# Softmax maxima as two rows of the stacked queries, a layer norm's affine folded into the next weights, and a new order of the steps

## The chip, the cores and the metric

The kernel runs on one core of one Trainium2 chip. The metric is the device time in microseconds, the median of the runs; one further execution was profiled, and all rows below come from it.

## The reference

Eight images of 256 channels and 16 x 16 pixels pass three blocks. The window block (two window attentions, one of them on DCT coefficients, then a 1x1 and a 3x3 convolution and a batch norm over all images) is the first half of the kernel. What the change touches is the second half. There `t` is an image as 256 tokens of 256 channels:

```python
out = feat + relu(batchnorm(y))                     # per image, t = out as tokens
mu, var = t.mean(-1), ((t - mu) ** 2).mean(-1)
tn = (t - mu) / jnp.sqrt(var + EPS) * n3_w + n3_b   # the MLP's affine
h = jax.nn.gelu(tn @ fc1_w.T + fc1_b, approximate=False)
t = t + (h @ fc2_w.T + fc2_b)
# attention, 16 heads of 16, rotary, causal, on the layer norm of t
scores = jnp.einsum('bhqd,bhkd->bhqk', q, k) * scale
probs = jax.nn.softmax(jnp.where(causal, -jnp.inf, scores), axis=-1)
t = t + (probs @ v) @ w_out
# eight experts, the two best by the gate's logits, on the layer norm of t
t = t + sum(combine[:, e] * (x @ expert_w[e].T) for e in range(8))
```

## The kernel before

Products of float32 quality are made from float16 parts: each operand is split into a high part (a cast, on ScalarE) and a low part (operand minus high part, on VectorE or GpSimd), and three matmuls are summed (`split_products`, line 200).

`windows` is the first half, up to about 345 us. At three of its steps it scales and splits the weights of the second half in chunks (`act_weights`, `dve_weights`). `images` is the second half. Each engine has its own in-order program; semaphores join them. The order in which each engine meets the steps comes from one list, made by `image_order` out of two tables written by hand: `MLP_SLOT` and `IMAGE_SLOT`. An entry is a step's name and its lag in slots; the steps of a slot follow the table, and each engine takes from the list those steps that it has a part in.

The steps of the MLP for image c: `load` (batch norm, relu, sum with the input), `tokens` (transpose, statistics on VectorE, `deviation` on GpSimd), `mlp_normalise` (ScalarE, two activations), `mlp_channels` (transposes on TensorE; on ScalarE two affine activations with `n3w`, `n3b` into `wide`, then the high part), `mlp_low`, `widen` (fc1, gelu, split of the hidden values on ScalarE and GpSimd), `narrow` (fc2), `mlp_base` (adds the bias of fc2). All eight images' MLPs run ahead of the first `attend`; the first steps of the attention of images 0 to 2 are interleaved with the last of them ("the fill").

The attention of image c: `qkv_normalise`, `qkv_channels`, `qkv_low`; `rotate` j = 0, 1 (products for queries and keys, rotary parts `rot` and `turned` on VectorE); `stack`: GpSimd adds (`rot`, line 1277), ScalarE makes `rh`, GpSimd `rl` (line 1281), SP writes both to `rope_scratch` in HBM and reads them back with twelve transfers (line 946) into `qs[p]` and `ks[p]`, whose rows 0 to 47 then hold high, low and high parts; rows 48 to 79 are zero. `maxima` n = 0..11 makes masked scores of query rows in bank (1, 1) (lines 1051, 1054) and reduces them on VectorE (line 1367); one bank serves all twelve, so each waits for the reduce before it. `shifts` splits the maxima in two bf16 parts (three operations on VectorE) and transposes them; `shift_rows` copies them to `shift[p]`. `attend` gr = 0..3 makes the transposed scores of four heads in three banks; for each head it subtracts the maximum by a second product of a matrix of selectors `headb` with `shift` (lines 1077 to 1084); ScalarE takes Exp (line 1216). `split` makes the parts of the exponentials (ScalarE, and GpSimd at line 1287), `weigh` multiplies with the values. Then `out_channels`, `out_split`, `out_project`, `moe_statistics`, `moe_normalise`, `norm_channels`, `logits` (the gate) and `expert` 0 to 7.

In the steady slots an engine's list holds `attend` of image k, `maxima` of image k + 1, `rotate` and `stack` of image k + 2 and the experts of image k - 1. On TensorE a slot before reads: `shifts`, `qkv_channels`, `attend` 0, `out_project`, `maxima` 0, `attend` 1, `maxima` 1 and 2, `rotate` 0, `maxima` 3, `norm_channels`, `attend` 2, `logits`, `rotate` 1, and then experts, `maxima`, `weigh` and `values` in turns, up to `expert` 7, `weigh` 3, `out_channels`. GpSimd's list: `moe_statistics`, `split` 0, `split` 1, `stack`, `rotated_low`, `split` 2, `split` 3. ScalarE's: `attend` 0, `split` 0, `attend` 1, `moe_normalise`, `split` 1, `norm_channels`, `attend` 2, `logits`, `attend` 3, `stack`, `split` 2, `split` 3 and the rest. SP's: `stack` of k + 2, `store` of k - 1.

## Time and profile before

| | us |
|---|---|
| median of 3 runs | 778.35 |
| lowest, highest | 772.43, 779.28 |
| the profiled execution | 771.87 |
| its span, first to last instruction | 769.9 |
| TensorE (PE) busy | 631.3 |
| VectorE (DVE) busy | 498.6 |
| ScalarE (ACT) busy | 326.8 |
| GpSimd (POOL) busy | 208.5 |

Busy time is a sum over stages with different limits. The page of the profile also has a chain: the work that ended last, followed back step by step to what released it. The granted clock is the share of TensorE's full 2.4 GHz that it was given; it has two levels, 0.5 (1.2 GHz) and 1. Matmuls are pipelined, so where they follow each other their starts tell what one costs.

### The profile page before, as it was taken

To read this page: it belongs to the slowest core of one execution; us is meant where nothing else is said; L and a number is where in the kernel's file an instruction comes from. 1 tells how busy PE (TensorE), PEld (TensorE's weight loads), DVE (VectorE), ACT (ScalarE), POOL (GpSimd) and SP (SyncE) were. 2 spreads that over 40 slices of the span, in tenths; PEclk is the share of its full clock that TensorE was granted. 3 is DMA by queue.
4 is the path that set the end of the run, shared out by engine and by line. 5 is a ranking of instruction groups with operands and counts; after the bars stand their busy time and mean duration, and the time that the engine had idled before them with its cause. 6 is when DMAs were issued, how large, how long until landed. Compare 5 with 4: busy or idle time off the path is not lost.

```text
span 769.9 us, 20275 instructions
## 1 busy us (share of the span) xinstructions
PE 631.3 (82%) x8800; PEld 531.5 (69%) x8800; DVE 498.6 (65%) x1102; ACT 326.8 (42%) x510; POOL 208.5 (27%) x193
## 2 busy tenths in 40 slices
PE   6656999897979897782797766799989898989867
PEld 5545787786868686661685645677878787867655
DVE  3586877878787979314364353477767686857445
ACT  4334434444443444104895224463545445342610
POOL 1000000000000000004587334463737363533330
PEclk9858999999999999995998988799999999999988
DMA  7103110101010000002033031404041322320000
GB/s 267 52 27 103 35 39 16 39 15 39 16 39 2 3 2 3 1 1 68 29 70 62 7 59 12 69 15 70 30 56 37 48 45 40 54 31 15 2 14 14
DMA packets 28408, 29.77 MB, mean 39 GB/s; under 512 B 1952, under 2 KB 22688, under 8 KB 28192
## 3 DMA queue, kind: packets, MB, share of 16 engines
q1 hardware_dynamic: 28320, 28.49, 16.6%
q8 instruction: 69, 1.13, 0.6%
q14 instruction: 19, 0.16, 0.1%
HBM read 22.19 MB, written 6.29 MB: 37 GB/s over the span
## 4 chain that ended last, share of the span: by engine, by line
PE 21%; DMA 10%; DVE 7%; POOL 6%; ACT 6%; SPq 3%; issue 2%; DVEq 0%; POOLq 0%; ACTq 0%
PE ps L200 11%; DMA ks<-rope_scratch 8%; SPq L946 3%; DMA rope_scratch<-rl 2%; PE ps L1051 2%; POOL rot L1277 2%; PE ps L1077 2%; POOL rl L1281 2%; PE ps L1080 2%; DVE mx L1367 1%; PE ps L1099 1%; POOL hl L1273 1%; ACT wide L1187 1%; PE ps L1083 1%; PE ps L962 1%
## 5 line engine op out<-in xcount | busy, mean ns | idle before, releaser
L1287 POOL TENSOR_TENSOR e2l<-prob,e2h 128x1536 f16<-128x1536 f32 x32 | 98.9, 3102 | 26.4 <-ACT e2h L1222 26.2
L1367 DVE TENSOR_REDUCE mx<-ps 128x2 f32<-128x512 f32 (+1 forms) x96 | 65.5, 682 | 33.0 <-PE ps L1054 33.0
L200 PE MATMUL ps<-secondh,ch_moe 128*128 128x256 f16 (+1 forms) x320 | 82.7, 266 | 3.3 <-DVE cl_moe L1320 3.0
L200 PE MATMUL ps<-secondl,ch_moe 128*128 128x256 f16 (+1 forms) x320 | 83.0, 266 | 0.0
L200 PE MATMUL ps<-secondh,cl_moe 128*128 128x256 f16 (+1 forms) x320 | 82.9, 266 | 0.0
L506 PE MATMUL ps<-yh,wconvh 128*128 128x256 f16 x288 | 80.8, 280 | 2.3 <-DVE yl L802 2.3
L506 PE MATMUL ps<-yh,wconvl 128*128 128x256 f16 x288 | 80.8, 280 | 0.0
L506 PE MATMUL ps<-yl,wconvh 128*128 128x256 f16 x288 | 80.4, 279 | 0.0
L1216 ACT ACTIVATE prob<-ps 128x1536 f32<-128x1536 f32 x32 | 46.5, 1452 | 58.5 <-PE ps L1083 58.5
L632 POOL TENSOR_TENSOR rstd<-mv,eps 128x4 f32<-128x4 f32 x8 | 1.6, 201 | 256.4 <-DVE mv L684 256.4
L1457 DVE SCALAR_TENSOR_TENSOR acc<-ps,gate,acc 128x256 f32<-128x256 f32 x112 | 49.0, 479 | 21.9 <-PE ps L200 21.9
L1051 PE MATMUL ps<-ks,qs 80*128 80x128 f16 (+1 forms) x256 | 38.5, 254 | 26.1 <-DVE mx L1367 16.4
L580 ACT ACTIVATE prob<-prob 128x1024 f32<-128x1024 f32 x16 | 16.9, 1058 | 86.0 <-DVE prob L747 86.0
L1222 ACT ACTIVATE e2h<-prob 128x1536 f16<-128x1536 f32 x32 | 47.0, 1476 | 4.8 <-PE ps L1099 3.9
L1051 PEld LDWEIGHTS ps<-ks,qs 80*128 80x128 f16 x256 | 18.6, 100 | 39.8 <-DVE mx L1367 25.6
L1077 PE MATMUL ps<-qs,ks 80*128 80x256 f16 (+1 forms) x256 | 40.0, 260 | 2.3 <-DVE shift L1388 1.1
L1080 PE MATMUL ps<-shift,headb 128*128 128x256 bf16 (+1 forms) x256 | 39.8, 260 | 0.0
L572 ACT ACTIVATE qkh<-ps,sbqk 128x256 f16<-128x256 f32 x64 | 26.9, 471 | 27.6 <-PE ps L200 27.6
L1251 POOL TENSOR_TENSOR rstd<-mv,eps 128x2 f32<-128x2 f32 x24 | 4.7, 196 | 122.4 <-DVE mv L1314 122.4
L200 PEld LDWEIGHTS ps<-secondh,ch_moe 128*128 128x128 f16 x320 | 31.1, 99 | 9.0 <-DVE cl_moe L1320 3.8
L1138 ACT ACTIVATE ch_moe<-ps 128x512 f16<-128x512 f32 x16 | 9.5, 595 | 62.3 <-PE ps L962 62.2
L200 PE MATMUL ps<-xh,wqkh 128*128 128x256 f16 x128 | 35.0, 274 | 0.0
(217 smaller groups left out, 2082.5 us busy)
## 6 DMA issues: line engine op xcount, KB each, us to landing
weights_stage<-in_second SPq DMA_DIRECT2D x6, 684.0 KB, 4.4
qs<-rope_scratch SPq DMA_DIRECT2D x48, 64.0 KB
ks<-rope_scratch SPq DMA_DIRECT2D x48, 64.0 KB
weights_stage<-in_wconv SPq DMA_DIRECT2D x6, 384.0 KB, 4.3
xw<-in_xw SPq DMA_DIRECT2D x8, 256.0 KB, 2.7
xc<-in_xc SPq DMA_DIRECT2D x8, 256.0 KB, 2.6
rope_scratch<-rh SPq DMA_DIRECT2D x8, 256.0 KB, 2.3
rope_scratch<-rl SPq DMA_DIRECT2D x8, 256.0 KB, 2.4
```

The lines of the kernel that those rows point to most:

```text
L200: last = nc.tensor.matmul(out_ap, lhs[x], rhs[w], start=done == 0, stop=done == n - 1)
L506: last = nc.tensor.matmul(bank(p, 2 + oh)[:, 0:TOK], w["wconv"][:, c0:c0 + P], im[:, h, dy:dy + HW, dx:dx + HW], start=(tap, h, n) == (0, ...
L572: nc.scalar.activation(qkh[p][:, j, oh, :], bank(p, j)[:, oh * TOK:(oh + 1) * TOK], ACT.Identity, bias=sbqk[:, j * 2 + oh:j * 2 + oh + 1]) ...
L946: sp.dma_start(dst[p][r0:r0 + 8], src).then_inc(stacked[p], 16)
L1051: nc.tensor.matmul(to[:, m * keys:(m + 1) * keys], qs[p][:, gr * GH + h, q0:q0 + P], ks[p][:, gr * GH + h, 0:keys], start=m == 0, stop=False)
L1077: nc.tensor.matmul(to[:, n * width:(n + 1) * width], ks[p][:, gr * GH + h, k0:k0 + P], qs[p][:, gr * GH + h, q0:TOK], start=n == 0, stop=F ...
L1080: nc.tensor.matmul(to[:, n * width:(n + 1) * width], headb[:, gr * GH + h, :], shift[p][:, q0:TOK], start=False, stop=False)
L1216: nc.scalar.activation(prob[n % 2][:], bank(0, 0, 3), ACT.Exp, scale=SOFTMAX_SCALE).then_inc(exp2, 1)
L1222: nc.scalar.activation(eh[n % 2][:], prob[n % 2][:], ACT.Copy).then_inc(e2_hi, 1)
L1287: nc.gpsimd.tensor_tensor(el[n % 2][:], prob[n % 2][:], eh[n % 2][:], ALU.subtract).then_inc(e2_lo, 1)
L1367: nc.vector.tensor_reduce(mx[c % 2][:, q0 // P, h0:h0 + len(heads)], bank(1, 1).rearrange("p (h m) -> p h m", m=keys), op=ALU.max, axis=AX ...
L1457: nc.vector.scalar_tensor_tensor(acc[c % 2][:, t, :], back_bank(e)[:, t * C:(t + 1) * C], gate[:, t, e:e + 1], (t3 if e == 0 else acc[c % ...
```

## The change

1. `qs` and `ks` get two more rows. Rows 80 and 81 of `ks` hold the constant 2^15. VectorE makes from the transposed maxima two float16 rows per head, -max / 2^15 and what that leaves (`shift_high`, `shift_done`), and SP copies each with one transfer into row 80 or 81 of `qs[p]`. `attend` contracts over 82 rows and has no product with `headb` any more; `headb`, the splitting of the maxima and their operations are gone. `attend` 0 now waits for the two transfers (`shift_in`). `maxima` takes rows 0 to 79 as before.
2. The MLP's affine: the rows of the fc1 weights are multiplied by `n3w` when they are split in `windows`, and `n3b` goes through fc1 once into a bias `fc1bias`, with a load of the raw weights and eight matmuls of one column at the start of `images`. `mlp_channels` on ScalarE is only the high part, read from PSUM. `mlp_normalise` moves from ScalarE to VectorE, as one subtract-and-multiply, and two of GpSimd's small operations go.
3. Both tables of slots are new. In the steady slots TensorE's list becomes: `shifts`, `qkv_channels`, `expert` 7, `out_channels`, `out_project`, `attend` 0, `maxima` 0 and 1, `rotate` 0, `attend` 1, `maxima` 2, `norm_channels`, `maxima` 3, `attend` 2, `logits`, `rotate` 1, `maxima` 4, and then the rest in turns. ScalarE: `attend` 0, `split` 0, `moe_normalise`, `attend` 1, `norm_channels`, `attend` 2, `split` 1, `logits`, `stack`, `split` 2, `attend` 3. GpSimd keeps its order. SP: `shift_rows` of k + 1 comes after `stack` of k + 2. In the MLP the steps of an image are one slot closer together; in the fill, `stack` of image 1 comes ahead of `widen` of image 7 on GpSimd.

```diff
 MLP_SLOT = [
-    ("load", 0), ("widen", 4), ("mlp_normalise", 2), ("mlp_base", 2), ("mlp_low", 3), ("narrow", 5),
-    ("statistics", 5), ("tokens", 1), ("mlp_channels", 2)]
-FILL_FROM, FILL_SLOT, FILL_END = 4.25, 3.0, 30.75
+    ("load", 1), ("mlp_base", 3), ("statistics", 6), ("tokens", 2), ("widen", 4), ("mlp_channels", 3),
+    ("mlp_normalise", 2), ("mlp_low", 3), ("narrow", 5)]
+FILL_FROM, FILL_SLOT, FILL_END = 4.5, 2.75, 18.5
...
+                    for c0, c1_, by in scaled_parts(c, width):
+                        last = nc.scalar.activation(high[:, c0:c1_], stage[slot][:, c0:c1_], ACT.Identity, scale=by)
...
+            def shift_rows(c):
+
+                p = c % 2
+                freed(sp, weights2, (c - 1) * GROUPS)
+                sp.wait_ge(shift_done, c + 1)
+                for n in range(2):
+                    sp.dma_start(qs[p][KROWS + n:KROWS + n + 1], shift[n][p][:]).then_inc(shift_in[p], 16)
...
-                    pe.wait_ge(shift_done, c + 1)
+                    pe.wait_ge(shift_in[p], (c // 2 + 1) * 2 * 16)
...
-                    for n, h in enumerate(heads):
-                        nc.tensor.matmul(to[:, n * width:(n + 1) * width], headb[:, gr * GH + h, :],
-                                         shift[p][:, q0:TOK], start=False, stop=False)
...
-                for h in range(HALVES):
-                    nc.scalar.activation(wide[c % 2][:, h, :], bank(0, 1)[:, h * TOK:(h + 1) * TOK], ACT.Identity,
-                                         scale=col("n3w", h), bias=col("n3b", h)).then_inc(affine2, 1)
-                act.wait_ge(affine2, c * 2 + 2)
-                nc.scalar.activation(ch[MLP][c % 2][:], wide[c % 2][:, 0:2, :], ACT.Copy).then_inc(mlp_hi, 1)
+                nc.scalar.activation(flat(ch[MLP][c % 2]), bank(0, 1), ACT.Copy).then_inc(mlp_hi, 1)
...
+                    last = nc.vector.tensor_scalar(tn[MLP][c % 2][:, t, :], t1[c % IN_MLP][:, t, :],
+                                                   mv[MLP][:, c, t, 0:1], rstd[MLP][:, c, t:t + 1], ALU.subtract,
+                                                   ALU.mult)
...
+                nc.vector.tensor_scalar(shift[0][p][:], bank(1, 1)[0:L1H, 0:TOK], -1.0 / SHIFT, None, ALU.mult)\
+                    .then_inc(shift_high, 1)
+                dve.wait_ge(shift_high, c + 1)
+                nc.vector.scalar_tensor_tensor(shift[1][p][:], bank(1, 1)[0:L1H, 0:TOK], -1.0 / SHIFT, shift[0][p][:],
+                                               ALU.mult, ALU.subtract).then_inc(shift_done, 1)
```

## Rows read from the trace of the kernel before

**Rows 1.** The page's chain that ended last, by line: share of the span.
```profile
PE ps L200 11%; DMA ks<-rope_scratch 8%; SPq L946 3%; DMA rope_scratch<-rl 2%; PE ps L1051 2%; POOL rot L1277 2%; PE ps L1077 2%; POOL rl L1281 2%; PE ps L1080 2%; DVE mx L1367 1%; PE ps L1099 1%; POOL hl L1273 1%; ACT wide L1187 1%; PE ps L1083 1%; PE ps L962 1%
```

**Rows 2.** Busy time by stage: stretch, its length, engines' busy us, clock, DMA.
```profile
core 0: us, PE busy (x) PEld busy (x) DVE busy (x) ACT busy (x) POOL busy (x), PEclk, DMA share, GB/s
348.00:427.00 79.00, 52.22 (x398) 43.22 (x399) 36.23 (x89) 56.66 (x108) 50.49 (x75) 0.83 0.26 57
427.00:459.00 32.00, 24.11 (x183) 18.64 (x182) 16.58 (x38) 5.36 (x9) 11.19 (x16) 0.87 0.18 31
...
496.60:677.00 180.40, 169.48 (x2169) 143.87 (x2168) 133.78 (x336) 84.51 (x88) 90.20 (x50) 0.99 0.28 45
...
712.70:769.90 57.20, 42.47 (x472) 35.02 (x472) 26.89 (x78) 15.63 (x17) 14.80 (x12) 0.85 0.03 10
```

**Rows 3.** The chain inside one slot, 549 to 586: start us, us, what.
```profile
549.15 0.67 DVE turned L1353 x2
549.89 2.37 POOL rot L1277
...
555.63 2.64 DMA rope_scratch<-rl
...
562.33 10.30 DMA ks<-rope_scratch
...
572.68 0.40 PE ps L1051 x4
...
576.73 1.32 PE ps L200 x12
...
585.07 0.76 DVE turned L1353 x2
```

**Rows 4.** TensorE's instructions in order of time, one `attend` and the next `maxima`.
```profile
605.15 0.38 PE L1080 MATMUL ps<-shift,headb 128*128 128x256 bf16 x2
605.37 0.27 PE L1083 MATMUL ps<-laterb,identb 128*128 128x256 bf16 x1
...
608.97 0.40 PE L1051 MATMUL ps<-ks,qs 80*128 80x128 f16 x4 [0.80 <-DMA ks<-rope_scratch]
```

**Rows 5.** DMA issues: count, KB each, median us from issue to landing.
```profile
xc<-in_xc SPq DMA_DIRECT2D x8, 256.0 KB, 2.6
...
out<-acc SPq DMA_DIRECT2D x8, 256.0 KB, 4.9
```

**Rows 6.** The page's costliest groups: busy us, mean ns, idle before, releaser.
```profile
L1287 POOL TENSOR_TENSOR e2l<-prob,e2h 128x1536 f16<-128x1536 f32 x32 | 98.9, 3102 | 26.4 <-ACT e2h L1222 26.2
...
L1216 ACT ACTIVATE prob<-ps 128x1536 f32<-128x1536 f32 x32 | 46.5, 1452 | 58.5 <-PE ps L1083 58.5
```

**Rows 7.** ScalarE's groups of instructions in the MLP, 373 to 403 us.
```profile
L1143 ACT ACTIVATE tn_mlp<-t,centre,rstd 128x256 f32<-128x256 f32 x9 | 4.9, 585 | 0.0
L1177 ACT ACTIVATE wide<-ps,vec 128x256 f32<-128x256 f32 x8 | 4.1, 558 | 2.4 <-POOL hl L1273 2.4
```

**Rows 8.** GpSimd's groups of instructions in the MLP, 373 to 403 us.
```profile
L1273 POOL TENSOR_TENSOR hl<-wide,hh 128x1024 f16<-128x1024 f32 x5 | 10.7, 2133 | 9.4 <-ACT hh L1190 9.4
L1254 POOL TENSOR_TENSOR rstd<-rstd,half 128x2 f32<-128x2 f32 x7 | 5.8, 834 | 0.5
L1267 POOL TENSOR_TENSOR t<-t,fc2b 128x512 f32<-128x512 f32 x4 | 5.1, 1270 | 0.0
```

**Rows 9.** VectorE's normalisation in the window half, a group of instructions.
```profile
L694 DVE TENSOR_SCALAR xn<-xw,mv,rstd 128x256 f32<-128x256 f32 x16 | 5.9, 410 | 5.2 <-POOL rstd L634 5.2
```

**Rows 10.** GpSimd in order of time in the fill.
```profile
442.26 2.35 POOL L1277 TENSOR_TENSOR rot<-rot,turned 128x1024 f32<-128x1024 f32 x1
```

**Rows 11.** Busy time by stretch near 720 us, columns as in rows 2.
```profile
719.00:722.00 3.00, 1.28 (x6) 1.15 (x7) 0.00 (x0) 3.00 (x5) 2.86 (x3) 0.74 0.00 0
722.00:725.00 3.00, 3.00 (x34) 2.30 (x31) 0.69 (x1) 0.79 (x3) 3.00 (x2) 0.69 0.00 0
```

More of the change, by code:

```diff
@@ L34 @@
 CST = {}
-for _name, _n in (("ident", P), ("dct", P), ("idct", P), ("dcsum", WTOK), ("causal", P), ("later", P), ("head", L1H), ("before", 64),
+for _name, _n in (("ident", P), ("dct", P), ("idct", P), ("dcsum", WTOK), ("causal", P), ("later", P), ("before", 64),
                   ("cos", TOK), ("sin", 2 * TOK)):
@@ L157 @@
 MLP_SLOT = [
-    ("load", 0), ("widen", 4), ("mlp_normalise", 2), ("mlp_base", 2), ("mlp_low", 3), ("narrow", 5),
-    ("statistics", 5), ("tokens", 1), ("mlp_channels", 2)]
-FILL_FROM, FILL_SLOT, FILL_END = 4.25, 3.0, 30.75
+    ("load", 1), ("mlp_base", 3), ("statistics", 6), ("tokens", 2), ("widen", 4), ("mlp_channels", 3),
+    ("mlp_normalise", 2), ("mlp_low", 3), ("narrow", 5)]
+FILL_FROM, FILL_SLOT, FILL_END = 4.5, 2.75, 18.5
 IMAGE_SLOT = [
-    ("out_project", 1), ("store", 2), ("moe_statistics", 1), ("split", 0, 0), ("maxima", -1, 0), ("attend", 0,
-    1), ("maxima", -1, 1), ("maxima", -1, 2), ("moe_normalise", 1), ("rotate", -2, 0), ("split", 0, 1),
-    ("maxima", -1, 3), ("norm_channels", 1), ("attend", 0, 2), ("logits", 1), ("rotate", -2, 1), ("expert", 1,
-    0), ("attend", 0, 3), ("stack", -2), ("maxima", -1, 4), ("weigh", 0, 0), ("expert", 1, 1), ("rotated_low",
-    -2), ("maxima", -1, 5), ("split", 0, 2), ("expert", 1, 2), ("weigh", 0, 1), ("maxima", -1, 6), ("expert", 1,
-    3), ("maxima", -1, 7), ("split", 0, 3), ("expert", 1, 4), ("maxima", -1, 8), ("values", -2), ("maxima", -1,
-    9), ("weigh", 0, 2), ("expert", 1, 5), ("maxima", -1, 10), ("expert", 1, 6), ("maxima", -1, 11),
-    ("qkv_normalise", -3), ("expert", 1, 7), ("weigh", 0, 3), ("out_channels", 0), ("shifts", -1),
-    ("shift_rows", -1), ("out_split", 0), ("qkv_channels", -3), ("attend", -1, 0), ("qkv_low", -3)]
@@ new lines @@
+    ("split", 1, 3), ("qkv_channels", -2), ("expert", 2, 7), ("out_split", 1), ("out_channels", 1), ("qkv_low",
+    -2), ("out_project", 1), ("moe_statistics", 1), ("attend", 0, 0), ("maxima", -1, 0), ("store", 3), ("split",
+    0, 0), ("maxima", -1, 1), ("rotate", -2, 0), ("moe_normalise", 1), ("attend", 0, 1), ("maxima", -1, 2),
+    ("norm_channels", 1), ("maxima", -1, 3), ("attend", 0, 2), ("split", 0, 1), ("logits", 1), ("stack", -2),
+    ("rotated_low", -2), ("rotate", -2, 1), ("maxima", -1, 4), ("expert", 1, 0), ("weigh", 0, 0), ("split", 0,
@@ L173, in image_order @@
+    2), ("expert", 1, 1), ("attend", 0, 3), ("maxima", -1, 5), ("expert", 1, 2), ("maxima", -1, 6), ("weigh", 0,
+    1), ("maxima", -1, 7), ("expert", 1, 3), ("values", -2), ("expert", 1, 4), ("maxima", -1, 8), ("expert", 1,
+    5), ("maxima", -1, 9), ("qkv_normalise", -3), ("expert", 1, 6), ("maxima", -1, 10), ("weigh", 0, 2),
+    ("maxima", -1, 11), ("weigh", 0, 3), ("shift_rows", -1), ("shifts", -1)]
 def image_order():
@@ L808, in weights @@
                     dve.wait_ge(weights_high, n + 1)
-                    nc.vector.scalar_tensor_tensor(low, stage[slot][:, 0:width], S, high, ALU.mult,
-                                                   ALU.subtract).then_inc(weights_split, 1)
+                    if c == 2:
+                        dve.wait_ge(n3_set, 1)
+                    for c0, c1_, by in scaled_parts(c, width):
+                        last = nc.vector.scalar_tensor_tensor(low[:, c0:c1_], stage[slot][:, c0:c1_], by,
+                                                              high[:, c0:c1_], ALU.mult, ALU.subtract)
+                    last.then_inc(weights_split, 1)
             def conv(c, oh):
@@ L877, in images @@
         eh, el = pair("e2h", [P, GW], f16), pair("e2l", [P, GW], f16)
-        mx, mxh = pair("mx2", [P, TILES, L1H]), one("mx2h", [P, TILES, L1H], bf16)
-        mxs = one("mx2s", [P, TILES, 2, L1H])
-        shift = pair("shift", [P, TOK], bf16)
-        headb = one("headb", [P, L1H, P], bf16)
+        mx = pair("mx2", [P, TILES, L1H])
+        shift = [pair(f"shift{part}", [L1H, TOK], f16) for part in "hl"]
         rs = one("rs2", [P, 2 * GH])
@@ L1128, in expert @@
                 token_product(back_bank(e), MOE, "wexp", e * 2 * C, C).then_inc(expert_done, 1)
+            pe.wait_ge(fc1_raw, 16)
+            for m in range(4):
+                for h in range(HALVES):
+                    last = nc.tensor.matmul(bank(1, 1)[:, m:m + 1], prob[0][:, h * HID + m * P:h * HID + (m + 1) * P],
+                                            col("n3b", h), start=h == 0, stop=h == HALVES - 1)
+            last.then_inc(fc1_fold, 1)
             run({"tokens": tokens, "mlp_channels": mlp_channels, "widen": widen, "narrow": narrow,
@@ L1293, in _ @@
                 nc.gpsimd.memset(vh[n][:], 1.0).then_inc(ones_set, 1)
-            for p in R2:
-                nc.gpsimd.memset(shift[p][:], 0.0).then_inc(shift_set, 1)
             pool.wait_ge(half_set, 3)
```

92 lines of the change are left out of this document (47 added, 45 removed), and 4 rows, old and new, of the table ln.

## The prediction

> **What bounds the kernel now.** I read the page's chain first [rows 1]. It mixes TensorE products with two transfers and VectorE, ScalarE and GpSimd steps, so no single engine sets the end everywhere. The table of busy time by stage comes next [rows 2]. The window half (0 to 348 us) is hardly touched and I leave it alone. From 348 us there are four stages: the MLP pipeline up to the first stacked image (427 us), the fill up to the first `attend` (459 us), slots of one image each (459 to 677 us; six slots, 218 us, 36.3 us a slot), and the last two images (677 to 769.9 us). In the steady slots TensorE is busy 169 of 180 us at a granted clock of 0.99. That looks like a TensorE bound, and a reader could stop there.
>
> The chain inside one slot says more [rows 3]. `turned` of image k+2 ends at 549.8; then come `rot` (2.37 us), its high part and its low part (ends 555.6), the spill to HBM, twelve loads into `qs`/`ks`, and at 572.63 they land. TensorE starts the next image's `maxima` 0.05 us later. `turned` of the next image ends at 585.8, one slot on. So 22.8 us from `turned` to landing plus 13.2 us from landing to the next `turned` make 36.0 us, the slot. In another slot TensorE visibly waits for such a landing, 0.80 us at 608.97 [rows 4]. TensorE and this loop are both at their limit: taking TensorE work out helps only if it lies in the 13.2 us, or if the loop shortens too.
>
> **The change, part by part.**
>
> *The shift matmuls.* Bank by bank `attend` has two or four products of `headb`; the first pair holds the stream from 605.15 to 605.37, 0.22 us [rows 4]. Three banks make 0.66 us, 32 `attend` steps 21 us. In the slots that end with a landing this is slack, apart from those ahead of `turned` in the loop. In the last two images nothing is stacked any more: 8 attends x 0.66 = 5.3 us come off there.
>
> *The rows that replace them.* `shift_rows` on VectorE becomes two operations of 16 rows in place of one of 32 and the three small ones in front: nothing net. But SP now has to copy both results into `qs`, behind its wait for `shift_done`, and behind that on SP's queue stand the next `store` and the next image's spill (not ready yet, so not delayed). The wait that matters is TensorE's: `attend` 0 waits for the copies, and in the new order it stands ahead of `maxima` 0. By my count below they are issued some 31 us after the slot's `attend` 0, when the twelve loads of the next image are still on their way (they land at 36.9). Do they overtake? The trace has a transfer in that position: the store of `acc`, issued while the twelve loads are out, takes 4.9 us to land against 2.6 us for `xc` with the same 256 KB [rows 5]. It ends with the loads. So I let the copies land 0.3 us behind the loads, and `attend` 0 (1.1 us without its shifts) stands behind them and ahead of `maxima` 0. Lower bound: no waiting, 0; upper bound: the copies need time of their own behind the loads, where twelve loads need 14.3 us from the first issue to the landing, about 1 us each [rows 3], so 2 us.
> The Trainium skill (page "DMA: Bandwidth & Descriptors", section "Why a DMA increments its semaphore by 16 and not by 1") says that a DMA from SP is spread over the largest number of engines, up to 16, that divides the slowest dimension of both sides. By that the loads (8 rows) use 8 engines, and a copy of 16 head rows into one row uses 16, or one if the target is seen otherwise; no row here shows which. Page and rows agree that a copy ends behind the loads; with one engine the sum would take the upper bound.
>
> *The order inside the slot.* I count the new order from the landing of the copies, with durations of the old trace (a product of 12 matmuls 1.31 [rows 3], `maxima` 0.33 or 0.44 and its reduce 0.68, Exp 1.45 and GpSimd's split 3.10 [rows 6], ScalarE's split 1.47). Landing 0; `attend` 0 to 1.15; Exp 0 to 2.9; `maxima` 0 and, after the wait for its reduce, 1 to 2.9; `rotate` 0 to 4.2; `attend` 1 to 5.3. ScalarE does split 0 (to 4.4) and the normalisation (to 5.5) before Exp 1 (to 7.0), so `attend` 2, which now follows after two short `maxima`, starts at 7.1; gate logits end at 8.8, `rotate` 1 at 10.1. The gate steps on VectorE need 3 us, and the gate's Exp now stands behind split 1 on ScalarE (to 11.4), 0.3 us more. `turned` ends at 13.9. GpSimd's split 1 runs until 14.5 and holds `rot` by 0.7 us. Then from `rot` to the landing as before, 22.4 us (mean over the slots; 22.7 in [rows 3]), so 36.9, and 0.3 for the copies: 37.2 us. Before: 36.3. Over six slots 6 x 37.2 = 223.2 against 218.1: **+5.1 us**. A cheaper `attend` on the path is used up by putting it whole ahead of `maxima` 0. TensorE's own work alone would allow about 35.9 us, because `out_project` now follows `out_channels` directly and waits 1.6 us for the split between them, and `maxima` 0 and 1 stand next to each other.
>
> *The MLP.* Between 373 and 403 us ScalarE makes four images (eight affine instructions, two an image [rows 7]), 7.5 us each, and is nearly never idle. The change takes from it two normalisations (0.585 each) and two affines (0.558 each): 2.2 us an image [rows 7]. Next in line is GpSimd: `hl` 2.13, `t` 1.27 and two sets of small steps around a 0.83 us power [rows 8] make 6.4 us; the change removes two of the small ones, 5.9. VectorE gets the normalisation; its own TENSOR_SCALAR of this shape costs 0.41 [rows 9], 0.8 us an image on an engine about half idle here. TensorE needs about 6.2. I take 6.6 us an image (5.9 to 7.4 the bounds): four images stand ahead of the one whose `widen` releases the first `rot` on GpSimd, 4 x 0.85 = 3.4 us, and about 3 us come from the pipeline, one step shorter: first `maxima` at 420.2, 6.5 us earlier. Then `rot` of image 1, which waits for `hl` of image 7 until 442.3 [rows 10], comes ahead of that `widen`: from first `maxima` to the landing 33.7 us, where it is 39.9. But the first `attend` now waits for this landing: 420.2 + 33.7 + 0.4 = 454.3 against 458.9, **-4.6 us**.
>
> *The folding itself.* Three pieces in place of one in one window's weight step are four instructions more; spread over one window of eight on two engines I bound them at 0 to 1 us. A 512 KB load and eight one-column matmuls ahead of the first image, against the `headb` copy and two memsets removed there: 0, at most +3. Both taken as 0.
>
> *The end.* From the last but one image's `attend` 0 to the end 92.9 us [rows 2]: -5.3 for the shifts, -1.3 for the waits between `weigh` 3 and `out_channels` that `expert` 7 now covers: **-6.5 us**.
>
> **Sum.** -4.6 + 5.1 - 6.5 = -6.0 us on the span of 769.9 (771.87 for that execution). The median shown is 6.5 us above it; I carry the difference over: 778.35 - 6 = **772**.
>
> **Rivals.**
> *B: the copies do not hold the loop.* If they land before the loads, or the waits that I count on ScalarE and VectorE shrink, a slot takes 35.9 us or a little less: 8 us less over six slots, -14 to -20, **761** (758 to 764). For it: removed work of 2.6 us a slot and TensorE busy 94% [rows 2]. Against: [rows 5].
> *C: the clock falls at each slot's start.* TensorE would be idle 1.6 us at `out_project` and about 0.9 us at `attend` 0. Where it was busy 1.28 of 3 us (719 to 722), the granted clock went to the lower of its levels, 1.2 GHz, and stayed there into the next 3 us, at means of 0.74 and 0.69, which is 1.6 + 1.9 us at that level [rows 11]; the steady slots stand at 0.99, 2.4 GHz nearly throughout [rows 2]. Such a spell costs half its 3.4 us, in the loop. Six times that: +10 on my sum, **782**. It needs the two idle stretches close together in most slots.
> The Trainium skill, page "TensorE: Matmul & The Clock Gate" (section "HAM oscillation — how this bites in real kernels"), describes the same pattern, a short wait for DMA in every round of a loop.
> *D, the other side: the copies take time of their own.* If each adds 1 us behind the loads, in seven slots, +14 on my sum: **787**, slower than before. It decides from about 1 us per slot above my 37.2 on top of a lost clock spell, or 2 us alone. For it: the loads still need 10.3 us after the last issue, so each transfer's time in the queue is real [rows 3]. Against: a copy is 8 KB where a load is 64 KB.
>
> **How the numbers follow.** My forecast 0.37, B 0.33, C 0.15, D 0.15. About 1% (7.8 us) is what a measurement here can tell from no change. Faster by over 1% (under 770.6): nine tenths of B and a third of mine, 0.43. Slower (over 786.1): half of D and a part of C with errors in the MLP term, 0.17. The rest 0.40. The likeliest case alone spans 765 to 780; the range goes to the others, **755 to 787**.
>
> **What would show each step.** Shift products gone: 1.1 us for an `attend`. `attend` 0 waiting for the copies' transfer, and starting with the landing of the loads, spacing 37.2 us; in B the spacing is 36 or less and TensorE waits for the loads at `maxima` 0. First `attend` near 454 us. In C a granted clock under 0.95 in the steady slots. In D `attend` 0 starts 1 us or more after the loads. Wrong from the ground would be a spacing near 33 us, which means the waits I count do not exist.

## The result, and the profile after

The changed kernel takes 810.92 us (median of 4 runs, 804.26 to 817.79), the kernel before 775.39 us beside it: a ratio of 1.0436, 95% interval 1.0369 to 1.0504. It is slower by 4.4%. The profiled execution of the changed kernel spans 812.0 us, that of the kernel before 769.9: the two traces lie 42.1 us apart, the medians 35.5.

The first lines are its busy time by stage: MLP, fill, then one line for each image from its `attend` 0 to the next, and the last image (the columns are those of [rows 2]).

```profile
core 0: us, PE busy (x) PEld busy (x) DVE busy (x) ACT busy (x) POOL busy (x), PEclk, DMA share, GB/s
352.11:430.55 78.44, 53.98 (x408) 45.53 (x409) 44.19 (x104) 40.79 (x75) 46.12 (x60) 0.83 0.29 65
430.55:463.01 32.46, 24.99 (x186) 19.05 (x187) 17.87 (x38) 7.62 (x12) 9.77 (x13) 0.83 0.26 42
463.01:500.84 37.83, 26.67 (x291) 19.44 (x291) 17.11 (x36) 15.00 (x14) 17.44 (x10) 0.71 0.24 36
500.84:545.22 44.38, 36.80 (x402) 28.86 (x403) 29.35 (x65) 16.69 (x18) 18.05 (x11) 0.86 0.23 31
545.22:585.29 40.07, 34.62 (x402) 27.93 (x403) 27.46 (x60) 16.69 (x18) 18.01 (x10) 0.91 0.24 41
...
712.28:751.56 39.28, 31.57 (x363) 25.00 (x364) 27.00 (x56) 13.78 (x13) 13.60 (x8) 0.87 0.04 14
751.56:812.00 60.44, 40.65 (x430) 32.34 (x427) 31.35 (x77) 15.58 (x17) 14.84 (x12) 0.83 0.03 10
```

Most of the loss is in the slots: 31.1 of the 42.1 us lie in five of them, 4.1 ahead of the first `attend` and 6.8 in the last two images. The first slot, which has no gate in it, is as long as before (37.8). The next five take 44.4, 40.1, 41.9, 44.4 and 40.7, a mean of 42.3, where the kernel before has 36.1 (the same marks in its trace; 35.8 in the slots at the full clock). TensorE's instructions are fewer (402 in place of about 435), but they are stretched: 36.8 us busy at a clock of 0.86. And TensorE is idle 7.6 us in such a slot, before about 2 us. What it waits for, over five slots' time of the changed kernel (500 to 712 us, which takes in the wait that ends at 500.8):

```profile
engine line waited for: us in total, times, longest us
PE ps L1077 <- DVE mx L1396: 17.5, 21, 1.9
PE ps L1101 <- DMA qs<-shiftl: 10.2, 4, 3.7
PE ps L201 <- DVE cl_moe L1340: 9.0, 10, 1.6
```

L1101 is `attend`, L1077 `maxima`, the third `out_project`. The second and third lines I had foreseen as waits, the third in its size. The first line was 4.6 us in the slots before, and the timeline of one slot shows where VectorE was late:

```profile
start us, us, engine line op out<-in xcount [idle before <-releaser]
556.44 1.48 ACT L1242 ACTIVATE e2h<-prob 128x1536 f16<-128x1536 f32 x1
557.34 0.29 DVE L1460 TENSOR_REDUCE rank<-cmp 128x16 f32<-128x128 f32 x1
557.81 0.21 ACT L1256 ACTIVATE gate<-gate 128x16 f32<-128x16 f32 x1
558.05 3.10 POOL L1309 TENSOR_TENSOR e2l<-prob,e2h 128x1536 f16<-128x1536 f32 x1 [5.18 <-ACT e2h L1242]
558.13 3.06 DVE L1462 SCALAR_TENSOR_TENSOR gate<-rank,gate 128x16 f32<-128x16 f32 x1 [0.50 <-ACT gate L1256]
561.22 0.17 DVE L1463 TENSOR_REDUCE g<-gate 128x2 f32<-128x16 f32 x1
561.62 0.17 DVE L1465 SCALAR_TENSOR_TENSOR gate<-gate,g 128x16 f32<-128x16 f32 x1
561.83 0.69 DVE L1378 TENSOR_TENSOR rot<-ps,cst 128x512 f32<-128x512 f32 x1
562.44 0.74 DVE L1382 TENSOR_TENSOR turned<-ps,cst 128x256 f32<-128x256 f32 x2
563.26 2.35 POOL L1299 TENSOR_TENSOR rot<-rot,turned 128x1024 f32<-128x1024 f32 x1 [2.11 <-DVE turned L1382]
```

A product of 16 numbers a partition takes 3.06 us. It begins 0.08 us behind GpSimd's split 1 (3.10 us) and ends 0.04 us behind it. All products on this line of the changed kernel, and then the same line of the kernel before, where split 1 came earlier and never met them (median 3058 against 176 ns):

```profile
L1462 DVE SCALAR_TENSOR_TENSOR gate<-rank,gate x8: 175/3058/3067, 516.1 to 797.5; 128x16 f32<-128x16 f32 x8
```
```profile
L1442 DVE SCALAR_TENSOR_TENSOR gate<-rank,gate x8: 175/176/176, 511.9 to 755.9; 128x16 f32<-128x16 f32 x8
```

So `turned`, which opens the loop of [rows 3], is late by 2.9 us. The other wait, ahead of `attend` 0, ends with the landing of the two copies of the shift rows. At its longest it is 3.75 us:

```profile
627.18 0.61 PE L1101 MATMUL ps<-qs,ks 82*128 82x256 f16 x2 [3.75 <-DMA qs<-shiftl]
```

The five slots end with 2.14, 0, 3.75, 2.23 and 0.92 us of it, a mean of 1.8. Around the longest the granted clock falls. This is the clock table of the changed kernel in steps of 3.4 us (the columns as above):

```profile
619.10:622.50 3.40, 1.84 (x17) 1.51 (x16) 2.39 (x5) 0.85 (x2) 0.00 (x0) 1.00 0.77 100
622.50:625.90 3.40, 0.94 (x9) 0.59 (x7) 1.69 (x5) 0.00 (x0) 0.36 (x2) 0.99 0.67 66
625.90:629.30 3.40, 2.12 (x12) 1.48 (x13) 0.00 (x0) 0.00 (x0) 0.90 (x3) 0.50 0.07 25
629.30:632.70 3.40, 2.61 (x14) 1.59 (x13) 1.38 (x2) 3.01 (x3) 0.00 (x0) 0.50 0.00 0
632.70:636.10 3.40, 3.40 (x20) 2.52 (x19) 1.35 (x3) 0.90 (x2) 3.09 (x1) 0.50 0.00 0
636.10:639.50 3.40, 2.88 (x26) 1.87 (x23) 1.98 (x3) 2.02 (x3) 0.00 (x0) 1.00 0.00 0
```

TensorE was busy 1.84 and then 0.94 of 3.4 us, with the wait for `out_project` and the wait for the copies close together; then the clock stands at 0.50 (1.2 GHz) for 10.2 us, the last 3.4 of them fully busy, before it is back at 2.4 GHz. In the slot that begins there TensorE is busy 36.8 us, where it was 31.9 in the slot before with nearly the same instructions. It is the pattern of [rows 11], now inside the steady slots.

### The profile page after: what moved, and what is told of

Read it like the earlier page. It is cut to its first block, busy times and chain, and to the rows that moved or that the text cites. A ratio compares the mean times of both kernels' runs of the same rounds, so it can differ in the third digit from the quotient of the medians.

```text
span 812.0 us, 19758 instructions
## 1 busy us (share of the span) xinstructions
PE 640.4 (79%) x8560; PEld 526.2 (65%) x8560; DVE 529.9 (65%) x1104; ACT 309.5 (38%) x481; POOL 203.3 (25%) x175
## 4 chain that ended last, share of the span: by engine, by line
PE 27%; DVE 12%; DMA 6%; ACT 4%; issue 4%; POOL 2%; SPq 1%; DVEq 0%; ACTq 0%; POOLq 0%
PE ps L201 15%; DMA qs<-shiftl 4%; PE ps L1077 3%; DVE mx L1396 3%; DVE gate L1462 3%; PE ps L1101 2%; PE ps L1120 2%; PE ps L1080 2%; DVE acc L1477 2%; PE ps L1104 1%; DMA ks<-rope_scratch 1%; ACT e2h L1242 1%; DVE turned L1382 1%; DVE gate L1465 1%; ACT prob L1236 1%
## 5 line engine op out<-in xcount | busy, mean ns | idle before, releaser
L201 PE MATMUL ps<-secondh,ch_moe 128*128 128x256 f16 (+1 forms) x320 | 86.6, 278 | 20.8 <-DVE cl_moe L1340 14.9
L201 PE MATMUL ps<-secondh,cl_moe 128*128 128x256 f16 (+1 forms) x320 | 86.9, 278 | 0.0
L201 PE MATMUL ps<-secondl,ch_moe 128*128 128x256 f16 (+1 forms) x320 | 86.7, 278 | 0.0
L1077 PE MATMUL ps<-ks,qs 80*128 80x128 f16 (+1 forms) x256 | 42.9, 276 | 41.2 <-DVE mx L1396 34.7
L1077 PEld LDWEIGHTS ps<-ks,qs 80*128 80x128 f16 x256 | 19.9, 106 | 57.0 <-DVE mx L1396 47.0
L201 PEld LDWEIGHTS ps<-secondh,ch_moe 128*128 128x128 f16 x320 | 32.4, 103 | 31.4 <-issue 12.4
L1101 PE MATMUL ps<-qs,ks 82*128 82x256 f16 (+1 forms) x256 | 39.5, 271 | 15.4 <-DMA qs<-shiftl 13.5
L1101 PEld LDWEIGHTS ps<-qs,ks 82*128 82x128 f16 x256 | 23.9, 108 | 23.3 <-DMA qs<-shiftl 12.7
L201 PEld LDWEIGHTS ps<-secondh,cl_moe 128*128 128x128 f16 x320 | 32.3, 103 | 5.6 <-issue 0.3
L201 PEld LDWEIGHTS ps<-secondl,ch_moe 128*128 128x128 f16 x320 | 32.6, 103 | 5.1
```

The source lines that it names most:

```text
L201: last = nc.tensor.matmul(out_ap, lhs[x], rhs[w], start=done == 0, stop=done == n - 1)
L1077: nc.tensor.matmul(to[:, m * keys:(m + 1) * keys], qs[p][0:KROWS, gr * GH + h, q0:q0 + P], ks[p][0:KROWS, gr * GH + h, 0:keys], start=m == ...
L1101: nc.tensor.matmul(to[:, n * width:(n + 1) * width], ks[p][:, gr * GH + h, k0:k0 + P], qs[p][:, gr * GH + h, q0:TOK], start=n == 0, stop=F ...
```

## Experiments

| kernel | median us | ratio to before | 95% interval | mean of slots 1 to 5 |
|---|---|---|---|---|
| changed | 810.92 | 1.0436 | 1.0369 to 1.0504 | 42.3 |
| e1 old arithmetic, new order | 823.4 | 1.0603 | 1.0559 to 1.0647 | 42.8 |
| e2 new arithmetic, old order | 809.65 | 1.0416 | 1.0381 to 1.0450 | 40.5 |
| e3 split 1 behind the stack | 799.12 | 1.0261 | 1.0211 to 1.0312 | 41.5 |
| e4 before, with split 1 late | 805.26 | 1.0368 | 1.0297 to 1.0438 | 39.9 |
| e5 copies from ScalarE's queue | 815.65 | 1.0457 | 1.0363 to 1.0552 | 42.8 |
| e6 split 1 behind the logits | 787.07 | 1.0129 | 1.0027 to 1.0231 | 38.6 |
| e7 loads of sixteen rows | 778.84 | 1.0032 | 0.9981 to 1.0082 | 38.5 |
| e8 before, loads of sixteen rows | 766.94 | 0.9861 | 0.9804 to 0.9918 | 35.9 |
| e9 e6 and e7 together | 753.24 | 0.9712 | 0.9642 to 0.9782 | 35.4 |
| e10 e2 with e7's loads | 794.13 | 1.0268 | 1.0194 to 1.0341 | 40.1 |
| e11 normalisation back on ScalarE | 809.2 | 1.0446 | 1.0342 to 1.0550 | 40.7 |
| e12 e9, `attend` 0 earlier | 766.32 | 0.9898 | 0.9774 to 1.0022 | 37.9 |
| e13 gate's sums in PSUM | 787.25 | 1.0178 | 1.0054 to 1.0302 | 38.4 |

Ratios compare with runs of the kernel before on the same chip (medians 774.5 to 779.8). Slots are measured from `attend` 0 to `attend` 0 in the profiled execution.

### The two halves of the change (e1, e2)

e1 is the kernel before with the new tables alone (`shifts` kept ahead of `shift_rows`), e2 the changed kernel with the old tables.

> The old arithmetic (shifts as a product of head rows, the MLP's affine on ScalarE) in the new order; nothing is left out. Theory P (port): in the changed kernel each slot lost 6.2 us, 3.1 of it because split 1 on GpSimd (e2l<-prob2,e2h, 3.10 us) now runs at the same time as VectorE's gate products, of which one then takes 3.06 us in place of 0.175. The new order alone brings this with it: 3 us in each of the slots with a gate, so at least 18 us on the images; without copies of shift rows nothing else is added, and the MLP keeps its old work: 790 to 802. Rival Q (copies): the slots lost their time to the two DMAs that bring the shift rows behind the twelve loads; without them the new order costs nothing: 770 to 782, and no slot longer than 36.5 us.

> The new arithmetic (copied shift rows, folded affine) in the old order, in which split 1 comes early and attend 0 stands ahead of the last products of a slot; nothing is left out. Theory P: no VectorE product of the gate meets GpSimd's split 1, so none takes over 0.3 us. But attend 0 stands where the loads of the stack are still on their way (in the old kernel it starts at 604.92 and PE waits for those loads until 608.97 afterwards), so the copies land at about 609.4 and attend 0 is pushed by 4.5 us, of which its own 3 us are paid again behind the wait: 3 to 4 us a slot, 18 to 24 on the images, less up to 6 on the MLP: 785 to 800. Rival Q, with the copies as the whole cause of the 6.2 us a slot: 805 or more. Rival R (the copies are hidden wherever they stand): 770 to 775.

e1 shows the collision without any copies: its gate product takes 3060 ns in the median. It missed its range of 790 to 802 upwards, since the MLP loses too (from the end of the windows to the first `maxima` 88.1 us, against 80.5 before and 79.8 in the changed kernel) and `shifts`, with its three VectorE operations, makes TensorE wait 5.9 us in five slots. e2 has no collision at the gate (no product over 178 ns). It came above its range too, at 810, because TensorE waits for the copies more than I counted:

```profile
PE ps L1101 <- DMA qs<-shiftl: 20.1, 5, 6.0
```

The number is rival Q's, but its reading, the copies as the whole cause, is not: e1 has no copies and loses more. So each half alone costs 4 to 6%, for different reasons. Old and new order are equally bad for the new arithmetic.

### The collision (e3, e4, e6, e13)

e3 edits the new table of slots, with split 1 going behind the stack,

```diff
-    ("attend", 0, 2), ("split", 0, 1), ("logits", 1), ("stack", -2), ("rotated_low", -2), ("rotate", -2, 1),
+    ("attend", 0, 2), ("logits", 1), ("stack", -2), ("rotated_low", -2), ("split", 0, 1), ("rotate", -2, 1),
```

and e4 the table of the kernel before:

```diff
-    ("split", 0, 1), ("maxima", -1, 3), ("norm_channels", 1), ("attend", 0, 2), ("logits", 1),
+    ("maxima", -1, 3), ("norm_channels", 1), ("attend", 0, 2), ("split", 0, 1), ("logits", 1),
```

> The changed kernel with one step moved: ScalarE's and GpSimd's split 1 goes from ahead of the gate's logits to behind the stack and the rotated low part; nothing is left out. Theory P: the gate's products take 0.18 us each again, rot on GpSimd does not wait for split 1 and starts about 3 us earlier, the stack's loads start 3 us earlier, and each slot with a gate is shorter by 3.1 to 4 us: 784 to 792. Rival Q (copies behind loads): the slot's length is set by the copies of the shift rows landing with the loads' end; as the loads go out earlier, the copies are earlier too, but the VectorE products have no part in it: with equal lengths of the gate's chain 808 to 812. Rival C (the clock falls because of other stalls): 805 to 812.

> The kernel before, old arithmetic and old order, with one step moved: split 1 goes from ahead of maxima 3 to directly ahead of the logits, as it stands in the changed kernel; nothing is left out. Theory P: GpSimd's split 1 now overlaps VectorE's products of the gate; one of them takes about 3 us and rot on GpSimd starts 3 us later, so the loads land 3 us later and every slot with a gate is longer by 2.5 to 3.3 us: 792 to 800. Rival (the move costs only one ScalarE operation, 0.3 us, ahead of the gate's Exp): 776 to 779.

e4 puts the collision into the kernel before, and nothing else: +27 us, more than the 15 to 23 expected. Three of its slots run at the full clock and take 38.15 us, 2.3 more than before; in two others the clock falls as well (41.6 and 43.5 us), and the span holds 5 us in the window half that this edit can't have caused (see below). e3 gained 12 us and not the 19 to 27 expected, because the wait only moved. Over five slots, the first line of its waits:

```profile
PE ps L1120 <- POOL e2l L1309: 23.3, 5, 4.7
```

`weigh` 1 now stands 4.7 us for the late split 1. No wait for the copies is left: TensorE now comes so late to `shifts` that the copies are issued when the loads have landed (590.02 against 587.41 in one slot), and there each lands in 1.9 us or less. e6 puts split 1 between: after the gate's Exp, ahead of the stack.

```diff
-    ("attend", 0, 2), ("split", 0, 1), ("logits", 1), ("stack", -2),
+    ("attend", 0, 2), ("logits", 1), ("split", 0, 1), ("stack", -2),
```

> The changed kernel with split 1 one step later, directly behind the gate's logits instead of ahead of them; nothing is left out. With split 1 behind the stack PE stood 4.66 us for split 1 of GpSimd, ahead of weigh 1 (611.5 to 616.17), where before the shift of the step it stood for attend 0: the wait was moved, not removed. Theory P: here the gate's products are free of GpSimd (0.18 us each), rot starts about 1 us behind turned instead of about 0.8 us behind a product 3 us late, and weigh 1 finds split 1 done: PE's idle time falls from 7.7 to about 5 us a slot: 788 to 798, below the 799 of the step behind the stack. Rival: the copies' wait of 3.75 us stays as long as it is, so that the slot gains only what the wait for attend 0 gives: 800 to 810.

It came at 787, a touch under theory P's range; the copies' wait stays (9.5 us in five slots). Its two slots at the full clock read:

```profile
540.45:575.96 35.51, 31.49 (x402) 26.41 (x403) 25.68 (x65) 16.81 (x18) 18.10 (x10) 1.00 0.25 47
575.96:614.11 38.15, 31.49 (x402) 26.42 (x403) 27.72 (x70) 16.81 (x18) 19.11 (x13) 1.00 0.28 43
```

The same work, the same clock; the second ends with 3.11 us of waiting for the copies, the first with 0.48. The slots differ by just that, 2.6 us: what TensorE waits for the copies goes onto the slot whole.

All three edits move work. e13 moves none; it changes where one input of the two products lies (and lets `expert` 1 wait until the gate is done):

```diff
+                rank_p = back_bank(1)[:, 32:32 + TILES * EXPERTS].rearrange("p (t e) -> p t e", t=TILES)
+                g_p = back_bank(1)[:, 64:64 + 2 * TILES]
-                step(nc.vector.tensor_reduce(rank[:], pairs(cmp), op=ALU.add, axis=AX), 5)
+                step(nc.vector.tensor_reduce(rank_p, pairs(cmp), op=ALU.add, axis=AX), 5)
...
-                step(nc.vector.scalar_tensor_tensor(gate[:], rank[:], 2.0, gate[:], ALU.is_lt, ALU.mult), 6)
+                step(nc.vector.scalar_tensor_tensor(gate[:], rank_p, 2.0, gate[:], ALU.is_lt, ALU.mult), 6)
```

> The changed kernel, its order untouched, with the rank and the sums of the gate kept in free columns of the logits' PSUM bank in place of SBUF, so that each of the two products that ran into GpSimd's split 1 has one input in PSUM; expert 1 waits until the gate is done; nothing is left out. Theory P (both engines want the same port only when the product has two inputs in SBUF): the products take 0.2 us although split 1 still runs at the same time; rot on VectorE comes about 3 us earlier, rot on GpSimd about 2 us: 790 to 803. Rival N (any work of VectorE waits while GpSimd runs this split, or the 3 us are a wait for something else): the products, or the reductions behind them, still take 3 us: 807 to 815.

```profile
630.05 0.20 ACT L1256 ACTIVATE gate<-gate 128x16 f32<-128x16 f32 x1
630.29 3.10 POOL L1309 TENSOR_TENSOR e2l<-prob,e2h 128x1536 f16<-128x1536 f32 x1 [6.85 <-ACT e2h L1242]
630.37 0.17 DVE L1464 SCALAR_TENSOR_TENSOR gate<-ps,gate 128x16 f32<-128x16 f32 x1 [0.45 <-ACT gate L1256]
631.00 0.17 DVE L1467 SCALAR_TENSOR_TENSOR gate<-gate,ps 128x16 f32<-128x16 f32 x1
631.21 0.69 DVE L1378 TENSOR_TENSOR rot<-ps,cst 128x512 f32<-128x512 f32 x1
```

The overlap is the same (the product begins 0.08 us behind split 1), and it takes 0.17 us. All eight take 174 to 176 ns. The time falls by 24 us against the changed kernel. The rival that any work of VectorE waits there is out.

The Trainium skill states this: page "SBUF — State Buffer", section "Who interferes with whom": a VectorE instruction with two SBUF inputs contends with a GpSimd instruction that reads SBUF, and the later one blocks for the whole of it. By that rule, read before, the product had to take what was left of split 1; these rows agree to 0.04 us. My sum used free durations for both engines.

### The copies (e5, e7, e8, e9, e10, e12)

In e5 ScalarE issues the two copies behind split 3.

```diff
-                    sp.dma_start(qs[p][KROWS + n:KROWS + n + 1], shift[n][p][:]).then_inc(shift_in[p], 16)
+                    nc.scalar.dma_start(qs[p][KROWS + n:KROWS + n + 1], shift[n][p][:]).then_inc(shift_in[p], 16)
```

> The changed kernel with the two copies of the shift rows issued by ScalarE's DMA queue, directly behind split 3 and ahead of the old first step of a slot, in place of SyncE's; nothing is left out. PE stood 3.75 us ahead of attend 0 (623.44 to 627.18) because the copies landed with the loads' end. Theory K (the queue): the copies stand behind twelve loads in SyncE's queue; from a queue of their own they land about 2 us after their issue, attend 0 starts about 3 us earlier in each of seven slots and some falls of the clock go: 784 to 794. Rival L (the engines): the packets of both queues share the same DMA engines, which the loads keep busy; the copies land as late as before, and ScalarE loses its issues besides: 808 to 816.

From issue to landing (least, median, most): the changed kernel, then e5, then e9, where the loads are short.

```profile
DMA to landing us min/median/max: 1.8/2.7/7.2
```
```profile
DMA to landing us min/median/max: 1.8/2.7/7.3
```
```profile
DMA to landing us min/median/max: 1.8/1.9/1.9
```

A queue of its own changes nothing; the engines behind the queues are what is shared. The Trainium skill says so (page "DMA: Bandwidth & Descriptors", section "Issuing engines are not separate DMA queues"), and these rows agree. e7 shortens the loads themselves, by another order of q's and k's channels, so that one transfer brings sixteen contiguous rows:

```diff
-                        for j in range(2):
-                            src = scratch[p, part, qk * 2 + j].rearrange("(h d) t -> d h t", h=L1H)
-                            r0 = n * L1D + j * 8
-                            sp.dma_start(dst[p][r0:r0 + 8], src).then_inc(stacked[p], 16)
+                        src = scratch[p, part, qk * 2:qk * 2 + 2].rearrange("j (d h) t -> (j d) h t", h=L1H)
+                        sp.dma_start(dst[p][n * L1D:(n + 1) * L1D], src).then_inc(stacked[p], 16)
...
-    order = lambda m: m.reshape(C, L1H, 2, 8).transpose(0, 2, 1, 3).reshape(C, C)
+    order = lambda m: m.reshape(C, L1H, 2, 8).transpose(0, 2, 3, 1).reshape(C, C)
```

> The changed kernel with the channels of q and k in the order (half, depth, head) in place of (half, head, depth), so that one DMA brings sixteen rows of 8 KB each in place of two that bring eight rows in pieces of 512 B: six loads for an image, not twelve; nothing is left out. Theory K: the twelve loads take 10.3 us because each reaches eight DMA engines; with sixteen the phase is 5 to 6 us, loads and copies land 4 to 5 us earlier, PE's 3.75 us ahead of attend 0 are gone: PE's idle time a slot falls from 7.7 to about 4 us, the falls of the clock become fewer: 784 to 794. Rival P (only the collision on VectorE counts, the copies' wait is a consequence of late rot): 800 to 811.

> The same loads of sixteen rows in the kernel before. There PE waits for the loads only 0.31 and 0.8 us a slot (572.37 to 572.68, 575.44 to 576.23), so at most 1 us a slot is to be had: 770 to 779. If the loads set the slot in a way that the waits don't show, 755 to 768.

> The changed kernel with both: split 1 directly behind the gate's logits, and loads of sixteen rows; nothing is left out. Each alone left one of the two waits: with split 1 moved, slots took 38.2 at the full clock with 3.1 us ahead of attend 0, and the one slot without that wait took 35.5; with the loads alone, slots took 37.8 with the collision. Theory P and K (two causes that add): slots of 35.5, first attend 0 at about 457, then 34 + 5 x 35.5 + 32.7 + 55: 754 to 764. Rival (one hides behind the other, so only the larger counts): 770 to 779.

e7 came at 779, 32 us under the changed kernel and below its range of 784 to 794; the waits for the copies are gone, the slots at the full clock take 37.8 to 38.0 with the collision still in them. How much of it is sixteen rows and how much the contiguous 8 KB was not taken apart. In e9 the six loads of an image take 7.8 us from the first issue to the last landing (585.40 to 593.24), in the changed kernel 13.4 us (571.36 to 584.78); over the eight images it is 7.8 to 8.4 against 12.3 to 15.0. In the kernel before the same edit gives 9 us (e8): its waits for the loads were small in the steady slots, which keep their 35.8 us, but the first images' loads stand on the path (the first `maxima` comes 3.4 us earlier, counted from the end of the windows, and the first slot is 6.4 us shorter). So the total falls into the second range of its expectation, but not by its reading: the loads don't set the slot there.

e9 is faster than both kernels. Four of its slots:

```profile
526.25:561.35 35.10, 31.32 (x404) 26.50 (x402) 26.18 (x65) 16.80 (x18) 18.08 (x10) 1.00 0.22 47
561.35:598.12 36.77, 32.99 (x405) 27.57 (x402) 26.34 (x65) 16.80 (x18) 18.08 (x10) 0.95 0.23 45
598.12:633.23 35.11, 31.34 (x405) 26.51 (x403) 26.18 (x65) 16.80 (x18) 18.09 (x10) 1.00 0.24 47
633.23:667.90 34.67, 30.89 (x401) 26.07 (x398) 25.58 (x64) 15.24 (x15) 18.09 (x10) 1.00 0.25 48
```

The two cures add: 24 us (e6) and 32 us (e7) make 56; together they give 58. At the full clock a slot of the new kernel costs 35.1; the collision adds 2.7 (e7: 37.8), and the copies add what TensorE waits for them, a mean of 1.8 in the changed kernel (two slots of e13 at the full clock agree: 36.8 us with 1.7 of wait, 37.5 with 2.7). That makes 39.6. Its slots have a mean of 42.3, and their clock is below 1; the last 2.7 us are what is left for it, by subtraction. Slot by slot 4.5, 2.3, 0.3, 4.4 and 1.9 us are left, and TensorE stood at 1.2 GHz for 12.4, 6.8, 1.3, 12.3 and 6.8 us of them.

Two tries at the order around `attend` 0 failed.

> The new arithmetic in the old order, with loads of sixteen rows; nothing is left out. In this order attend 0 stands 3.6 to 3.7 us behind the shifts' transposes with nothing but qkv's transposes between (583.83 to 587.54 without the new loads). Theory L (that wait is the copies' place behind the loads): with the loads done early it goes to 1 us or less, PE's busy time a slot is 31.5 in place of 33.8, idle 3: slots of 34.5: 748 to 758. Rival T (the wait is the time that transposes, two VectorE operations and a DMA take one after another, whatever the loads do): it stays at 3 us or more, slots of 37: 764 to 776.

> The kernel with both cures (split 1 behind the logits, loads of sixteen rows) and one step moved: attend 0 goes ahead of out_project; nothing is left out. There PE stood 1.56 us ahead of out_project in every slot (558.48 to 560.04), waiting for the low part of the transposed output, while the copies of the shift rows had landed at 595.07 and attend 0 only began at 598.12. Theory O (the place of attend 0 is what is left): its products fill the 1.56 us, and 1.0 us more behind maxima 0 may go: slots of 33.5 in place of 35.1: 740 to 748. Rival T (attend 0 now comes before the copies have landed and waits instead): 750 to 757.

e10 takes 794, beyond either range, and the direction is the rival's: TensorE still waits for the copies with loads of sixteen rows:

```profile
PE ps L1099 <- DMA qs<-shiftl: 12.3, 4, 3.1
```

That is the time of transposes, two VectorE operations and a transfer of 1.9 us, one after another; with 0.6 us of other work between (the transposes of `qkv_channels`), no faster load helps. Each such gap brought spells at the lower clock (0.87 to 0.94 in these slots). e12 moves `attend` 0 ahead of `out_project` in e9, where I had read the copies as landed. It lost 13 us and came above both of its ranges. `attend` 0 now waits for them (1.47 us in the slot shown), and the next wait grew, since the reduce of `maxima` 0 stands behind the statistics of the experts' input on VectorE, which now come later:

```profile
569.64 0.69 DVE L1430 SCALAR_TENSOR_TENSOR t<-ps,z 128x512 f32<-128x512 f32 x1 [2.16 <-PE ps L201]
570.37 0.75 DVE L1327 BATCH_NORM_STATS2 st<-t 128x6 f32<-128x256 f32 x2
571.23 0.25 DVE L1332 BATCH_NORM_AGGREGATE mv<-st 128x2 f32<-128x6 f32 x2
571.39 0.66 DVE L1394 TENSOR_REDUCE mx<-ps 128x4 f32<-128x512 f32 x1
572.11 0.39 PE L1075 MATMUL ps<-ks,qs 80*128 80x256 f16 x2 [2.13 <-DVE mx L1394]
```

### The MLP (e11)

```diff
-                    last = nc.vector.tensor_scalar(tn[MLP][c % 2][:, t, :], t1[c % IN_MLP][:, t, :],
-                                                   mv[MLP][:, c, t, 0:1], rstd[MLP][:, c, t:t + 1], ALU.subtract,
-                                                   ALU.mult)
+                normalise(c, MLP, t1[c % IN_MLP])
```

> The changed kernel with one edit undone in the MLP: the normalised tokens are made by ScalarE again (with GpSimd's three small operations for its bias), in the same place of the order; the folded affine stays, nothing is left out. In the changed kernel VectorE's two normalising operations took 0.41 us alone and 1.4 to 2.5 us in five of sixteen, where GpSimd was busy. Theory P (this overlap costs the MLP what the fold was to give): 2 to 5 us earlier at the first maxima, counted from the end of the windows: 806 to 811. Rival S (ScalarE sets the pace of the MLP, so its two operations of 1.08 us together come back): 5 to 8 us later: 814 to 820.

The totals can't tell (809.2 against 810.9). From the end of the windows to the first `maxima` e11 takes 82.1 us, the changed kernel 79.8, and e6 and e13, whose work up to there is the same in the same order, 77.5 and 79.2. That is 2.3 to 4.6 us later, where theory P had it earlier and S 5 to 8 later. So the move to VectorE gains a few us there, in spite of the overlaps; how much, one trace of e11 can't tell. The overlaps are real. The row is of the changed kernel, from the groups between 352 and 431 us:

```profile
L1351 DVE TENSOR_SCALAR tn_mlp<-t,mv,rstd 128x256 f32<-128x256 f32 x16 | 11.0, 725 | 8.5 <-POOL rstd L1274 8.5
```

A mean of 725 ns where thirteen of them take about 410, as this shape does in [rows 9]: three (not five, as the expectation has it) began behind a GpSimd instruction that was still running, and took 1.71, 2.14 and 2.43 us. One that began 0.14 us ahead of such an instruction took 406 ns.

## Why the prediction was wrong, step by step

- *What bounds the kernel.* The loop from `turned` to the landing was right, and it is what the collision lengthens. In the slot from 545.22 I counted `turned` ending 13.9 us behind the landing; it ended at 563.18, 18.0 behind. 2.9 of the 4.1 us are the product of L1462; the rest was not taken apart (TensorE stood at 1.2 GHz from 547.36 to 550.77 in it). From there to the next `attend` 0 it took 22.1, against 22.4 + 0.3.
- *The order inside the slot* is the step that failed: "The gate steps on VectorE need 3 us, and the gate's Exp now stands behind split 1 on ScalarE (to 11.4), 0.3 us more." I saw that split 1 moved up to the gate and priced it by ScalarE's queue, with GpSimd's split running free beside VectorE. They had not met in the old trace at that place. But it did show the effect elsewhere: `cl_mlp` (two inputs in SBUF) averaged 977 ns over eight, where six took 685, and two, begun during GpSimd's `hl` and `t`, 2167 and 1542. I did not ask why.

```profile
L1330 DVE TENSOR_TENSOR cl_mlp<-wide,ch_mlp 128x512 f16<-128x512 f32 x8 | 7.8, 977 | 0.0
```

- *The copies.* "0.3 us behind the loads" held: 0.4 in the slot above (585.19 against 584.78), 0.4 to 0.8 in five of the others and 1.3 in one, so rival D, with time of their own, did not come in most slots. The wait they cause, a mean of 1.8 us and 3.75 at most, is longer than the 0.9 I gave it. TensorE, 2.4 us lighter in a slot (31.5 busy at the full clock, e4 33.9), may simply reach `attend` 0 earlier than the loop allows; no run tests that by itself.
- *Rival C, the clock,* came in its mechanism, but on top of the collision and not in place of it; I had set it as a case apart. I counted 3.4 us a slot at 1.2 GHz and 1.7 us lost by them. It was 7.9 us a slot, and what is left for them in the slots' length is 2.7.
- *First `attend`*: 454.3 predicted, 463.0 measured. 4.4 us of the difference lie in the window half, which ended at 346.4 before and 350.7 after. That is not the change's, as far as the runs show: the window code of e4 is that of the kernel before and ended at 351.5; that of e11 is the changed kernel's and ended at 346.6.
- *The MLP* gained 0.7 us by the first `maxima` and not 6.5. The pace was right: from image 1 to image 4, counted at ScalarE's high part `ch_mlp`, 20.0 us, 6.7 an image, before 23.8. What failed is "about 3 us come from the pipeline, one step shorter". Image 1's `ch_mlp` comes 9.6 us behind image 0's, before 4.9, and so image 4's stands where it stood (45.0 us behind the windows' end, before 44.9). That is the new order's: 9.9 us in e1, 4.8 in e2. Which entry of the table does it stays open. 1.6 us more are the fold at the start (load and eight matmuls, which I put at 0 with a bound of 3): the first image's first product comes 9.5 us behind the windows' end, before 7.9. The two halves don't add up to the whole: from the windows' end to the first `maxima` the new order alone takes 88.1 us (e1), the new arithmetic alone 81.0 (e2), both 79.8, neither 80.5. The fill took 32.5 us against 34.1 counted.
- *The tail*: -6.5 predicted, +6.8 measured (99.7 against 92.9). The same two causes: without the collision it is 88.0 (e6), without either 84.8 (e9), -8.1. The collision is the larger part, 12.5 us (e7's 97.3 against e9): in two of the tail's gates the second product, L1465, is held too, for 2.61 us. The gain that I forecast was there, near its size, once both were gone.
- *The sum.* e9 against e8, both with loads of sixteen rows and neither with a collision, is 753 against 767. So what I expected the change to bring was there, and more, with split 1 one step later. The changed kernel is 58 us above e9. 9 of these the shorter loads give to the kernel before as well; some 49 are the two causes' with the clock they bring, and I had counted 5. Two slips in the working change nothing: D's 787 is 786 by its own terms (772 and 14), and ScalarE's 2.2 us an image are 2.3 by the rows.

## What to carry to other kernels

When a step is moved, list what each engine runs beside it afterwards, and price an overlap of VectorE and GpSimd with the memory of every input: a 0.18 us product with two SBUF inputs can cost the whole of a 3 us GpSimd instruction, and one input in PSUM makes it free. A small transfer that something waits for is as late as the large ones that are out when it is issued, whichever queue issues it; shorten those, or leave more work than its own chain needs ahead of the wait. TensorE's short waits can cost more than their length: of the five slots of the changed kernel, the four that ended with a wait for the copies, near the one for `out_project`, had the clock fall at that place, and the one without had not.
